# Weighted values of block-diagonal attention on the quarters of TensorE's array

## The reference

```python
W = cond_weights[condition]                    # (64, 32, 32), one matrix per sequence
h = einsum('bct,bcd->bdt', x, W)               # (64, 32, 512)
q, k, v = h @ Wq + bq, h @ Wk + bk, h @ Wv + bv   # inner width 4096 = 32 heads x 128
q, k = rms_norm(q, gq), rms_norm(k, gk)        # over all 4096
attn = softmax(einsum('bhqd,bhkd->bhqk', q, k) / sqrt(128))   # 32 x 32 per sequence and head
out = einsum('bhqk,bhkd->bhqd', attn, v)       # the weighted values
x = x + out @ Wo + bo
x = x + ffn(cond2(x))                          # quantised weight with LoRA, then 8 low-rank experts
```

## Time and profile before

| | us |
|---|---|
| median of 3 runs | 1615.69 |
| lowest and highest run | 1613.99, 1616.41 |
| the profiled execution's own time | 1615.28 |
| its span in the trace | 1613.7 |
| TensorE matmul busy in the span | 1591.6 |
| VectorE, ScalarE, GpSimdE busy | 1192.2, 715.6, 748.4 |

### The profile page before, as it was taken

How to read it: one execution, slowest core, us unless ns; L and a number is a source line. 1 busy time by engine, 2 the same in 40 slices (tenths; PEclk the granted TensorE clock), 3 DMA queues, 4 the chain that set the end, 5 groups by cost and what they waited for, 6 DMA issues and landing times.

```text
span 1613.7 us, 24939 instructions
## 1 busy us (share of the span) xinstructions
PE 1591.6 (99%) x9398; PEld 1403.9 (87%) x9398; DVE 1192.2 (74%) x1848; ACT 715.6 (44%) x1200; POOL 748.4 (46%) x531
## 2 busy tenths in 40 slices
PE   8999999999999999999999999999999999999998
PEld 7888888888888888887999999998888888888886
DVE  7788888888888888986388888976565656665652
ACT  7566656656666666665333333333331222222210
POOL 6466766767666666765234444443441111111100
PEclk9999999999999999999999999999999999999999
DMA  3111011101111011101333333345444242332330
GB/s 136 53 40 36 24 40 40 40 26 35 39 40 39 21 40 40 40 25 36 116 127 132 131 131 131 131 157 195 151 156 145 79 130 89 95 123 86 95 98 30
DMA packets 105863, 133.95 MB, mean 83 GB/s; under 512 B 6016, under 2 KB 88064, under 8 KB 105232
## 3 DMA queue, kind: packets, MB, share of 16 engines
q1 hardware_dynamic: 105280, 132.23, 24.8%
q10 hardware_dynamic: 464, 0.13, 0.0%
HBM read 86.20 MB, written 46.14 MB: 82 GB/s over the span
## 4 chain that ended last, share of the span: by engine, by line
PE 94%; DVE 4%; issue 1%; ACT 1%; DMA 1%; ACTq 0%; DVEq 0%
PE bank L558 37%; PE bank L760 22%; PE bank L567 18%; PE bank L715 7%; PE bank L656 4%; PE bank L644 3%; PE bank L815 1%; PE bank L798 1%; DVE accr L1370 1%; DMA vec<-in_vecs 1%; DVE xs_lo L1335 0%; DVE qreg L1369 0%; DVE sqst L1392 0%; PE bank L778 0%; PE bank L664 0%
## 5 line engine op out<-in xcount | busy, mean ns | idle before, releaser
L558 PE MATMUL bank<-xs_hi,wa 128*128 128x512 f32 x1792 | 586.3, 396 | 2.4 <-ACT snap L940 1.2
L1189 POOL TENSOR_TENSOR accr<-accr,sqst 128x512 f32<-128x512 f32 x248 | 371.2, 1509 | 220.8 <-ACT sqst L952 179.2
L558 PEld LDWEIGHTS bank<-xs_hi,wa 128*128 128x128 f32 x1792 | 337.1, 188 | 72.2 <-issue 4.7
L558 PE MATMUL bank<-xs_lo,wa 128*128 128x512 f32 x896 | 349.4, 390 | 0.0
L567 PE MATMUL bank<-wv,xs_hi 128*128 128x256 f32 x1792 | 327.9, 286 | 5.8 <-DVE wv L1282 3.6
L760 PE MATMUL bank<-ot,wo_main 128*128 128x512 f32 x1344 | 320.6, 394 | 0.0
L760 PEld LDWEIGHTS bank<-ot,wo_main 128*128 128x128 f32 x1344 | 249.2, 189 | 49.4
L567 PEld LDWEIGHTS bank<-wv,xs_hi 128*128 128x128 f32 x1792 | 282.8, 194 | 9.4 <-DVE wv L1282 4.3
L567 PE MATMUL bank<-wv,xs_lo 128*128 128x256 f32 x896 | 255.4, 285 | 0.0
L1593 DVE SCALAR_TENSOR_TENSOR ot<-bank,vec,ot 128x512 fp32r<-128x512 f32 x128 | 95.1, 750 | 187.6 <-ACT ot L1083 179.7
L1392 DVE COPY sqst<-bank 32x128 f32<-32x128 f32 x512 | 146.9, 287 | 96.8 <-PE bank L656 85.2
(11 more groups left out here) (186 smaller groups left out, 1900.9 us busy)
## 6 DMA issues: line engine op xcount, KB each, us to landing
sqst<-v_spill SPq DMA_DIRECT2D x63, 512.0 KB, 3.9
wraw<-in_wqk SPq DMA_DIRECT2D x32, 512.0 KB, 3.5
v_spill<-vo SPq DMA_DIRECT2D x64, 256.0 KB, 2.3
v_spill<-sqst SPq DMA_DIRECT2D x64, 256.0 KB, 2.3
score_spill<-sqst SPq DMA_DIRECT2D x32, 256.0 KB, 2.0
wraw<-in_wv SPq DMA_DIRECT2D x16, 512.0 KB, 5.1
wraw<-score_spill SPq DMA_DIRECT2D x16, 512.0 KB, 5.4
accr<-in_wo SPq DMA_DIRECT2D x16, 512.0 KB, 4.8
```

Source lines behind the costliest of these rows:

```text
L558: ins = pe.matmul(dst[:, :], wa[:, col:col + P], xpart[:, j - 1, kt, n * CH:(n + 1) * CH], start=(first and k == 0), stop=(k == 5), skip_g ...
L1189: pool.tensor_tensor(a, a, sq_slot(count), ALU.add).then_inc(acc_done, 1)
```

## The change

The 128x128 matrix of softmax weights is cut into halves: keys 0 to 63 with queries 0 to 63 (two sequences) and keys 64 to 127 with queries 64 to 127. The two other halves are zero and are left out. Each old matmul of 128 rows, 128 weight columns and 128 moving columns becomes four of 64, 64 and 64: r selects the half of the sequences (the rows of the array), d the half of the head width (the weight columns, and the partitions of the output). They come in the order h, t, d, r, so that four in a row lie on four different quarters of the array. Bank 4 now takes r = 0 and bank 5 takes r = 1, each for both heads; bank 6 is no longer used for this. pv(b) is one group and raises pv_done once; it waits for all of out_lo(b - 1). ScalarE and VectorE read each bank in two instructions of 128x256, and `ot` keeps its layout, in which the halves alternate in runs of 64. pv(0) stands as a whole after p7(95).

```diff
-        def pv_bank(b, h):
-            return bank[4 + (2 * b + h) % 3]
+        pv_bank = (bank[4], bank[5])
+
+        def pv_part(r, h):
+            return pv_bank[r][:, h * 256:(h + 1) * 256].rearrange("p (t n) -> p t n", t=TC)
+
+        def ot_part(o, r):
+            return o.rearrange("p (t r n) -> p r t n", t=TC, r=2)[:, r]
...
             def load_v(b):
                 if b >= 2:
-                    sp.wait_ge(pv_done, 2 * b - 2)
+                    sp.wait_ge(pv_done, b - 1)
...
-            def pv(b, h):
-                q = 2 * b + h
-                if h == 0:
-                    pe.wait_ge(ld_v[b % 2], 16 * (b // 2 + 1))
-                    pe.wait_ge(pt_ready, b + 1)
-                if q >= 3:
-                    pe.wait_ge(o_lo, q - 2)
-                elif q == 0:
+            def pv(b):
+                pe.wait_ge(ld_v[b % 2], 16 * (b // 2 + 1))
+                pe.wait_ge(pt_ready, b + 1)
+                if b >= 1:
+                    pe.wait_ge(o_lo, 2 * b)
+                else:
                     pe.wait_ge(c21_done, N_ST - 1)
-                elif q == 1:
                     pe.wait_ge(c12_done, N_ST - 1)
-                else:
-                    pe.wait_ge(c11_done, N_ST - 1)
-                for t in range(TC):
-                    ins = pe.matmul(pv_bank(b, h)[:, t * P:(t + 1) * P], values(b)[:, t, h * DH:(h + 1) * DH],
-                                    pt[:, b % 2, h, t, :], start=True, stop=True)
+                for h in range(2):
+                    for t in range(TC):
+                        for d in range(2):
+                            for r in range(2):
+
+                                rows = slice(r * 64, (r + 1) * 64)
+                                out = pv_bank[r][d * 64:(d + 1) * 64, (h * TC + t) * 64:(h * TC + t + 1) * 64]
+                                ins = pe.matmul(out, values(b)[rows, t, h * DH + d * 64:h * DH + (d + 1) * 64],
+                                                pt[rows, b % 2, h, t, r * 64:(r + 1) * 64], start=True, stop=True)
                 ins.then_inc(pv_done, 1)
...
                 if s + 1 < N_ST:
                     p1(s + 1)
-                else:
-                    pv(0, 0)
...
                 else:
-                    pv(0, 1)
+                    pv(0)
                 p4(s)
                 p3(s)
...
                 if b >= 1:
-                    pv(b, 0)
-                    pv(b, 1)
+                    pv(b)
                     project_out(b - 1)
...
-            def out_hi(b, h):
-                act.wait_ge(pv_done, 2 * b + h + 1)
+            def out_hi(b, r):
+                act.wait_ge(pv_done, b + 1)
...
-                act.activation(ot[:, b % 2, 0, h, :], pv_bank(b, h)[:, :], ACT.Identity,
-                               bias=vec[:, 2 * (b % NP) + h, 2:3], scale=1.0).then_inc(o_hi, 1)
+                for h in range(2):
+                    ins = act.activation(ot_part(ot[:, b % 2, 0, h, :], r), pv_part(r, h), ACT.Identity,
+                                         bias=vec[:, 2 * (b % NP) + h, 2:3], scale=1.0)
+                ins.then_inc(o_hi, 1)
...
                 if b >= 2:
-                    dve.wait_ge(pv_done, 2 * b - 2)
+                    dve.wait_ge(pv_done, b - 1)
...
-            def out_lo(b, h):
-                dve.wait_ge(o_hi, 2 * b + h + 1)
-                dve.scalar_tensor_tensor(out=ot[:, b % 2, 1, h, :], in0=pv_bank(b, h)[:, :],
-                                         scalar=vec[:, 2 * (b % NP) + h, 2:3], in1=ot[:, b % 2, 0, h, :].bitcast(F32),
-                                         op0=ALU.add, op1=ALU.subtract).then_inc(o_lo, 1)
+            def out_lo(b, r):
+                dve.wait_ge(o_hi, 2 * b + r + 1)
+                for h in range(2):
+                    ins = dve.scalar_tensor_tensor(out=ot_part(ot[:, b % 2, 1, h, :], r), in0=pv_part(r, h),
+                                                   scalar=vec[:, 2 * (b % NP) + h, 2:3],
+                                                   in1=ot_part(ot[:, b % 2, 0, h, :].bitcast(F32), r),
+                                                   op0=ALU.add, op1=ALU.subtract)
+                ins.then_inc(o_lo, 1)
```

More of the change, by code:

```diff
@@ L1071, in _ @@
                     act.activation(sc[0], sc[0], ACT.Exp).then_inc(sm_exp, 1)
-            def out_hi(b, h):
-                act.wait_ge(pv_done, 2 * b + h + 1)
-                if h == 0 and b == 1:
+            def out_hi(b, r):
+                act.wait_ge(pv_done, b + 1)
+                if r == 0 and b == 1:
                     act.wait_ge(v_stored[11], 16 * N_V)
                     act.wait_ge(v_stored[22], 16 * N_V)
-                if h == 0 and b >= 2:
+                if r == 0 and b >= 2:
                     if (b - 2) % NP == NP - 1:
```

## The result

The changed kernel takes 1590.61 us, the median of 4 runs (1589.63 to 1591.54), beside 1616.05 us for the kernel before: a ratio of 0.9845 with a 95% interval of 0.9828 to 0.9862. The forecast was 1588 us, with a range of 1560 to 1646. The profiled execution took 1590.28 us, its span is 1588.7 us, 25.0 us shorter than before.

The account below looks back on a forecast made before the run. TensorE, busy 99% of the span, was taken as the bound. From the profiled 1615.28 us, 30.4 saved in plain steps, 2 given back around the residual and 1 at the join made 1588 us, range 1560 to 1646.

Parts of the forecast that it names:

- The passes: Weighted-values matmuls of a step: 64 passes, four quarters working at once, cost 0.90 us instead of 1.79.
- In and out of the division: Changing the array's division twice in each output-stage step costs 0.40 us together.
- The plain step: Output-stage steps 2 to 63: each saves 0.49 us, 30.4 us over 62 steps.
- The drains: ScalarE's and VectorE's four shorter bank reads take 1.64 and 1.80 us, ending about 3 us after the last pass, hidden.
- The residual: Three places where VectorE is nearly full around the residual may stop TensorE: 0.7 us each, 2 us given back.
- The join: Where pv(0) moves behind p7(95) and pv(1) waits for out_lo(0): from -1 to +3 us, taken as +1.
- the forecast's own part: Whole-kernel range if the forecast holds: 1558 us (division changes free) to 1605 (they cost double in part); chance 0.70.
- Half the overlap: Rival for the weighted-values passes: at most two quarters work at once, 1.79 us a step, 1643 us; chance 0.15.
- A limit on starts of 0.028 us: Rival for the weighted-values passes: each start takes 0.028 us, giving 1.79 us a step and 1643 us; chance 0.05.
- No overlap: Rival for the weighted-values passes: one after another, 3.58 us a step, 136 us more, 1754 us; chance 0.04.
- The clock: Rival in every output-stage step: small passes bring a half-speed stretch, 1.7 us a step, 1693 us; chance 0.03.
- the drains did not become the bound: Rival: ScalarE and VectorE take over 5.4 us to finish out_lo, nearly nothing saved, within 0.2% of today; chance 0.03.

Follow-up runs that it names:

- e2: Changed kernel with row halves alone: 64 rows, all 128 weight columns, 64 moving columns, 32 passes a step; 1641.84 us.
- e3: Kernel before with weight columns halved alone: 128 rows, 64 weight columns, 128 moving columns, 32 passes a step; 1633.65 us.
- e1: Changed kernel with pv's loops reordered, d and r outermost, so sixteen passes in a row lie on the same quarter; 1732.76 us.
- e4: Changed kernel with the first of project_out's four blocks between head 0's and head 1's passes, so the array's division changes four times a step; 1620.4 us.
- e5: All of the change but the quarters: old full-array matmuls with the new banks, reads, waits and join; 1618.35 us, ratio 1.0018 to the kernel before.
- e6: Changed kernel with one DMA moved: the 1 MB second residual load issued in step 17 instead of step 14; 1586.15 us, ratio 0.9813 to the kernel before.
- e7: On top of e6, score products of both groups cut to diagonal 32x32 blocks on four column strips; 1555.95 us, ratio 0.9627.
- e8: Changed kernel with loops ordered d, h, t, r, so passes alternate between two row quarters, then the same on the other half; 1636.33 us.
- e9: Changed kernel with loops ordered t, d, r, h, so two matmuls in a row, four passes, lie on one quarter; 1597.12 us.

## Why the prediction was right, step by step

- **The passes.** Right. Reckoned 0.90 us a step with four quarters at once; measured 16 x 0.058 = 0.93. L668's eight passes were a fair model, and rows overlap like columns (e2, e3). The prediction named the rotation, but did not see how much hangs on the order of the loops: e1 costs 142 us against the changed kernel.
- **In and out of the division.** Right: 0.40 reckoned from L548, 6.76 - 24 x 0.227 - 0.93 = 0.38 measured in the step and 0.39 by doubling it (e4).
- **The plain step.** 0.49 us reckoned, 0.48 measured, 0.6 us less over 62 steps.
- **The drains.** Right: 1.57 and 1.66 us against 1.64 and 1.80 reckoned, out_lo done 2.8 us after the last pass against 3; e5 shows them free in plain steps.
- **The residual.** The weak step. I gave back 0.7 us at each of three places for a full VectorE. Two lost nothing (6.76 us at steps 33 and 49); step 17 took 11.08 us instead of 7.00 (7.48 less 0.48), 4.1 lost. The cause is not VectorE's own work, but a load, of which I wrote that shorter steps leave it less time and that it matters little at 43% of the DMA engines. That was the share of a plain step; ahead of step 17 it is 80%, and e6, with 40% there, gives most of the loss back. The trace of the kernel before showed it already, in the two steps ahead of its step 17 (columns as in the earlier trace rows):

```profile
1212.20:1219.50 7.30, 7.30 (x42) 6.31 (x42) 3.15 (x6) 1.37 (x2) 0.00 (x0) 1.00 0.96 318
1219.50:1226.70 7.20, 7.20 (x41) 6.28 (x40) 2.81 (x4) 1.38 (x2) 2.41 (x1) 1.00 0.67 189
```

- **The join.** Right: reckoned +1 us, measured +1.0. From the 2641st matmul of the values (1094.61 before, 1093.21 after) to the start of step 2 it is 19.82 us before and 20.77 after, and 20.78 and 20.84 in e6 and e7, which have the same join. The gap ahead of pv(1) is 4.26 us instead of 2.52, 1.7 longer where 1.8 was reckoned, and the stretch at half clock does double there, to 6.8 us:

```profile
1104.67 1.99 PE L722 MATMUL bank<-qreg 64*64 64x64 f32 x64 [4.26 <-DVE ot L1600]
```

- **The values, ahead of the change.** Not in the sum, and luck. Nothing is changed there, and the first matmul of the values starts at 756.18 in both kernels, yet the changed one reaches the 2641st 1.4 us sooner. Around and behind L668 the clock was at 0.50 for 6.8 us in the trace of the kernel before and for 3.4 in this one, first before, then after:

```profile
779.10:782.50 3.40, 3.40 (x18) 3.40 (x18) 0.69 (x1) 0.60 (x1) 0.00 (x0) 0.50 0.00 0
```

```profile
779.10:782.50 3.40, 3.40 (x30) 3.40 (x30) 1.47 (x4) 0.60 (x1) 0.00 (x0) 0.98 0.00 0
```

- **The end.** Not in the sum either. From the last L722 group to the end of the span it took 31.44 us where 30.66 - 0.48 = 30.18 was due. The trace shows 6.8 us at half clock there against 3.4 before; in e6, with 3.4 us of it again, the same stretch took 30.0 us. It changed from kernel to kernel with no edit near it; what decides it was not found.

The sum by the trace: 61 x 0.48 + 0.48 = 29.8 saved, 4.1 lost at step 17, 1.0 lost at the join, 1.4 gained in the values, 1.3 lost at the end, 24.8 us against the 25.0 measured. The forecast had 27.4 (30.4 - 2 - 1). Of what it was too high by, 2.1 us are the residual, mis-sized by half, and 0.6 the plain steps; the two stretches at half clock, which it could not know, cancelled by chance. Of the range, the low end of the forecast's own part is 2 us under its sum: 1615.3 - 55 is 1560, and not 1558, even with nothing given back.

- **The rivals.** Half the overlap did not come, but its size holds: e8 forces it and takes 1636 us where 1643 were reckoned (the period is 7.52 us, where 7.24 + 0.40 = 7.64 were reckoned). A limit on starts of 0.028 us is refuted by 15 ns here and 8.5 ns in e7. The prediction had only the loads of L668 against it; the single records of its passes, four starts from 776.191 to 776.211, say the same in the kernel before. So the Trainium skill's 25 ns ("TensorE: Matmul & The Clock Gate", section "Wait — 56ns, not 53.3ns?") does not hold across parts of the array either, by these rows. No overlap: e1 comes close to it with 3.4 us. The clock stayed at 1.00 in plain steps, and the drains did not become the bound.

## What to carry to other kernels

A block-diagonal fp32 matmul that is cut into more and smaller ones gained here only where both the weight columns and the moving columns shrank, where consecutive matmuls lay on different parts (with two in a row on one part at most), and where the passes saved outweighed about 0.4 us for going in and out of the division; a group of eight full passes was enough. Each half of the rows had a PSUM bank of its own here (one bank for both was not tried), which changed the waits, so plan the banks first. When a stage gets faster, look for the loads that just made it before: here one late load took a seventh of the 29.8 us that were due, and one moved DMA gave it back.

## What the runs showed of the hardware that I had not expected

- The second pass of an fp32 matmul does not hold up the next matmul on another part (starts in fours, 7 ns apart, with two passes to each matmul), and a run of four passes on one quarter is nearly free (e9: 1.30 us against 1.16 for 64 passes), while a run of sixteen serialises (e1: 3.40 us).
- Passes on different parts start 7 ns apart within a group, and 8.5 ns apart on average over the 32 passes of e7.
- TensorE ran at half clock for 6.8 or for 3.4 us with the same program: around and behind L668 in the kernel before and in the changed one (1.4 us), and at the end of the changed kernel and of e6 (31.4 against 30.0 us). A difference of about 1 us between two executions can be this alone.
